# Spreading two sums of absolute values over heads 1 to 11 and splitting the rounding of the second weight, in a transformer layer on one core

## The chip, the cores and the metric

The kernel runs on one core of a Trainium2 chip. The core has five engines that run their own instruction streams and meet only at semaphores: PE (TensorE, matrix products into PSUM), ACT (ScalarE, activations), DVE (VectorE, elementwise work and reductions), POOL (GpSimd, elementwise work in SBUF) and SP (SyncE, here only an issuer of DMAs). POOL and ACT can issue DMAs too. Sixteen DMA engines move the data. The metric is the device time of one execution in microseconds (us).

## The reference

One layer over four sequences of 512 tokens of width 512: attention with 16 query heads of size 32 that share one key and one value head, a residual with layer norm, a gated feed-forward block whose three weights are rounded to -1, 0 or 1, and a residual with layer norm again.

```python
q = rotary((x @ Wq + bq) by heads);  k = rotary(x @ Wk + bk);  v = x @ Wv + bv
attn = softmax(q @ k.T / sqrt(32));   x = layernorm(x + (attn @ v) @ Wo + bo)

def quantize(w):
    gamma = mean(abs(w))                       # over the whole 1408 x 512 matrix
    return clip(round(w / (gamma + 1e-8)), -1, 1)

hidden = sigmoid(x @ quantize(w1).T) * (x @ quantize(w2).T)
x = layernorm(x + hidden @ quantize(w3).T)
```

What matters here is `quantize`: the sum of absolute values over a whole weight has to be known before its first element can be rounded.

## The kernel before

**Sequences and heads.** Sequence 0 runs through its 16 heads in `first_heads()` of each engine. A head is four score tiles of 128 x 512 (PE, line 1309), four row minima (DVE, 1021), four exponentials (ACT, 723), sixteen turns of 128 x 128 blocks (PE, 1337) and four copies of the turned tiles out of PSUM, two on ACT (751) and two on DVE (1042); the turns and copies of head h-1 lie inside head h. Every four heads make a group, whose context is summed a head later (PE, 1366). Sequences 1 to 3 run in `heads(b)`, in 32 steps k, two to a head; a step makes two score tiles, and around them the tables `BESIDE` and `LAST_BESIDE` place everything else: projections of the next queries, keys and values, the output projection, and the feed-forward block of the sequence before (`up0` to `up10`, `dn0` to `dn3`). From sequence 1 on the probabilities are cut into two 16-bit halves (ACT 744, DVE 1034, the latter in `p_low`) and turned by DMA transposes, one to a step, that SP issues (line 467, `turn`). They leave from four slots: the exponentials of step k wait for the transpose of step k-4.

**Weights.** `stage[0]` holds w1, `stage[1]` w2, and `stage[2]` is the same memory as `stage[0]` and takes w3. Each weight goes through three steps. ACT sums absolute values in four pieces of 128 x 1408 (`abs_sum(i)`, line 760; i from 0 to 3 is w1, 4 to 7 w2, 8 to 11 w3). PE adds the four partial sums over the partitions (`total(n)`, 1394) and DVE makes the threshold of it (`thresholds(n)`, 894 to 899). POOL rounds the weight in four pieces of three instructions each (`round_weight(n, c)`, 541, 543, 545); each piece raises the semaphore `rounded` by one. The tables `ABS_AT` and `TOTAL_AT` name the heads of sequence 0 at whose end the pieces 0 to 7 and the totals 0 and 1 stand. Pieces 8 to 11 stand in steps 4 to 7 of sequence 1, and the third total after step 8.

**POOL** also does the rotations (`rotation`: cosines 522, sines 527, sum 530), adds the output bias to the input rows (`add_bias`, 563), makes the inverse deviations (551 to 558), and from sequence 1 on issues the DMAs that stack the high and low halves of a head's queries (`stack`, 422; four DMAs a head). In sequence 0 SP issues those stacks.

**SP** runs in one order. Behind the stacks of sequence 0 it waits for all eight pieces of w1 and w2, then issues the rows of x (`load_x(0)`, line 453) and w3 (488), and behind these stand the transposes of sequence 1:

```python
sp.wait_ge(rounded, 2 * PIECES)
load_x(0)
sp.dma_start(stage[2], w3).then_inc(w_ffn[2], 16)
...
turn(b, *divmod(k - 1, PAIRS))      # line 467, sequence 1 onwards
```

The order inside POOL, SP, ACT, DVE and PE is written out by hand; no scheduler changes it.

Of the kernel before, what the change touches and what calls it, by code (L numbers as in the profile page):

```python
# [56 lines left out]
PIECES = 4  # L57
# [5 lines left out]

FIRST_Q_AT = [3, 7, 11, 15]
FIRST_Q = [(0, 2), (0, 3), (1, 0), (1, 1)]
ABS_AT = [0, 1, 1, 2, 3, 4, 5, 6]
TOTAL_AT = [3, 7]
FIRST_POOL_ROTATES = ("q1", "q2", "q3")
ROUND = 1.5 * 2.0 ** 23

# [131 lines left out]
def layer(nc, xT, x, wq, small, wo, b_rows, w1, w2, w3, table, out):  # L202
    with ExitStack() as ctx:
# [309 lines left out]
        def _(pool):  # L513
# [55 lines left out]
            pool.wait_ge(lo_done, unit_count(0, "k") + 1)  # L569
            rotation(0, "q1")  # L570
            rotation(0, "q2")
            pool.wait_ge(thr_step, 2)
            for c in range(PIECES):
                round_weight(0, c)
            rotation(0, "q3")
            pool.wait_ge(thr_step, 2 * 2)
            for c in range(PIECES):
                round_weight(1, c)
            rotation(1, "q0")
            cosines(1, "k")  # L580
            stack(pool, 1, 0)
            add_bias(0, 0)
            add_bias(0, 1)
            sines(1, "k")
            add_bias(0, 2)
            add_bias(0, 3)
            for h in range(1, HPG - 1):
                stack(pool, 1, h)
            for b in range(1, B):
                stack(pool, b, 3)  # L590
                if b > 1:
                    inverse_std(b - 2, 1, 2)
                rotation(b, "q1")
                if b > 1:
                    inverse_std(b - 2, 1, 3)
                stack(pool, b, 4)
                stack(pool, b, 5)
                rotation(b, "q2")
                stack(pool, b, 6)
                inverse_std(b - 1, 0, 0)  # L600
                inverse_std(b - 1, 0, 1)
                stack(pool, b, 7)
                inverse_std(b - 1, 0, 2)
                inverse_std(b - 1, 0, 3)
                if b == 1:
                    pool.wait_ge(thr_step, 2 * 3)
                    round_weight(2, 0, 0)
                    round_weight(2, 2, 1)
                stack(pool, b, 8)
                stack(pool, b, 9)  # L610
                rotation(b, "q3")
                if b == 1:
                    round_weight(2, 1, 2)
                    round_weight(2, 3, 3)
                add_bias(b, 0)
                stack(pool, b, 10)
                add_bias(b, 1)
                stack(pool, b, 11)
                add_bias(b, 2)
                add_bias(b, 3)  # L620
                for h in range(12, H):
                    stack(pool, b, h)
                if b < B - 1:
                    rotation(b + 1, "q0")
                if b < B - 1:
                    inverse_std(b - 1, 1, 0)
                    stack(pool, b + 1, 0)
                    stack(pool, b + 1, 1)
                    inverse_std(b - 1, 1, 1)
                    rotation(b + 1, "k")  # L630
                    stack(pool, b + 1, 2)
# [571 lines left out]
        def _(pe):  # L1203
# [146 lines left out]
            def first_context(g, blocks):  # L1350

                for k in blocks:
                    if k == 0:
                        if g == 0:
                            pe.wait_ge(kv_drained, 3)
                        if g < 2:
                            pe.wait_ge(total_read, g + 1)
                        if g == 2:
                            pe.wait_ge(kv_drained, 5)
                        pe.wait_ge(ctx_done, g)  # L1360
# [26 lines left out]
            def total(n):  # L1387

                pe.wait_ge(abs_summed, (n + 1) * SUMS)
                pe.wait_ge(ctx_done, n if n < 2 else HG)  # L1390
                if n == 0:
                    pe.wait_ge(ones_set, 1)
                    pe.wait_ge(kv_drained, 3)
# [204 lines left out]
```

## Time and profile before

| | |
|---|---|
| time, median of 3 runs (lowest to highest) | 607.18 us (606.84 to 608.12) |
| time of the profiled execution | 605.79 us |
| span of its instructions | 604.0 us |
| PE busy | 546.0 us, 90% of the span |
| DVE busy | 470.7 us, 78% |
| ACT busy | 426.0 us, 71% |
| POOL busy | 303.4 us, 50% |
| granted TensorE clock, mean | 0.974 of full |

The profiled execution took 1.4 us less than the median, and its span leaves out 1.8 us around the first and the last instruction. Busy shares are means over stages with different limits. Sequence 0's heads end at about 119 us in the span; the stage of interest runs from there to about 200 us. All times below are microseconds from the start of the span unless a duration is meant.

### The profile page before, as it was taken

Reading aid. Unit: us, or ns where it says so; the run is one execution under the profiler, and the core shown is the slowest. Engines: PE = TensorE matmul, PEld = TensorE weight load, DVE = VectorE, ACT = ScalarE, POOL = GpSimd, SP = SyncE. Lnnn points to the kernel's source line nnn. Section 1 sums busy time; section 2 is a strip of 40 time slices with the busy share of each in tenths; the row PEclk is TensorE's granted clock in tenths of the full one; section 3 lists DMA queues with packets and bytes.
Section 4 is the critical chain, followed back from the end, with each engine's and each line's share of the span. In section 5 each row is a group of like instructions: output and inputs, shape, how many; then the busy total and the mean of one; then the engine's idle time right before and its main releaser. Section 6 shows DMA issues by size and latency. Waiting matters only on the chain.

```text
span 604.0 us, 9187 instructions
## 1 busy us (share of the span) xinstructions
PE 546.0 (90%) x2984; PEld 273.0 (45%) x2984; DVE 470.7 (78%) x635; ACT 426.0 (71%) x865; POOL 303.4 (50%) x398
## 2 busy tenths in 40 slices
PE   9777989899789798999899989999599999989993
PEld 5443545444344344445444445354344444444441
DVE  2867878889989698888899898799989897444433
ACT  2697767789978587686888897687989796233300
POOL 2219696838599633958457325897453400201011
PEclk9789999999999899999899999999799999999997
DMA  8680428249989778999999987999899989100001
GB/s 307 189 307 17 123 49 301 54 81 191 215 182 180 159 151 134 163 199 197 213 200 190 191 161 140 176 188 197 171 218 167 183 165 195 41 1 36 1 0 69
DMA packets 217119, 92.12 MB, mean 153 GB/s; under 512 B 204400, under 2 KB 205552, under 8 KB 216560
## 3 DMA queue, kind: packets, MB, share of 16 engines
q1 hardware_dynamic: 209952, 77.61, 62.3%
q0 software_dynamic: 6144, 12.60, 10.1%
q10 hardware_dynamic: 976, 1.33, 0.6%
q8 instruction: 24, 0.39, 0.3%
q14 instruction: 23, 0.19, 0.1%
HBM read 20.20 MB, written 4.19 MB: 40 GB/s over the span
## 4 chain that ended last, share of the span: by engine, by line
PE 57%; DVE 13%; issue 9%; POOL 8%; ACT 7%; DMA 3%; SPq 2%; POOLq 0%; ACTq 0%; DVEq 0%
PE a_ps L1281 10%; PE b_ps L1281 6%; PE c_ps L1382 6%; PE s_ps L1294 6%; PE a_ps L1212 5%; PE e_ps L1281 5%; PE s_ps L1326 4%; DVE p_all L1034 3%; PE c_ps L1366 3%; PE b_ps L1294 2%; DVE sh_sb L1027 2%; POOL q_st L422 2%; PE b_ps L1266 2%; PE a_ps L1294 2%; PE s_ps L1337 2%
## 5 line engine op out<-in xcount | busy, mean ns | idle before, releaser
L736 ACT ACTIVATE p_all<-s_ps,sh_sb 128x512 f32<-128x512 f32 x192 | 130.1, 683 | 58.0 <-DVE sh_sb L1027 57.4
L1027 DVE TENSOR_REDUCE sh_sb<-s_ps 128x2 f32<-128x1024 f32 x96 | 116.7, 1215 | 23.8 <-PE s_ps L1326 23.7
L1034 DVE SCALAR_TENSOR_TENSOR p_all<-p_all 128x1024 f16<-128x1024 f32 x96 | 131.0, 1364 | 3.1 <-ACT p_all L744 3.0
L744 ACT ACTIVATE p_all<-p_all 128x1024 f16<-128x1024 f32 x96 | 101.7, 1060 | 2.0
L1281 PE MATMUL a_ps<-late,q 128*128 128x512 f16 x352 | 83.5, 380 | 3.2 <-DVE late L974 1.7
L1326 PE MATMUL s_ps<-k_st,q_st 128*128 128x512 f32 x192 | 79.2, 494 | 2.7 <-ACT p_all L736 1.6
L551 POOL TENSOR_SCALAR rstd<-mv 128x1 f32<-128x1 f32 x32 | 9.2, 287 | 136.6 <-DVE mv L994 136.4
L422 POOL DMA_DIRECT2D q_st<-hi x96 | 49.5, 518 | 51.9 <-PE s_ps L1326 28.2
L1212 PE MATMUL a_ps<-xT_sb,wq_sb 128*128 128x512 f32 x104 | 51.9, 625 | 4.9 <-DVE late L1013 4.1
L1281 PEld LDWEIGHTS a_ps<-late,q 128*128 128x128 fp8e4 x352 | 31.8, 98 | 45.9 <-issue 7.4
L422 POOL DMA_DIRECT2D q_st<-lo x96 | 47.4, 498 | 9.6 <-DVE lo L937 9.3
L723 ACT ACTIVATE p_all<-s_ps,sh_sb 128x512 f32<-128x512 f32 x48 | 33.0, 693 | 21.6 <-DVE sh_sb L1021 21.6
L1326 PEld LDWEIGHTS s_ps<-k_st,q_st 128*128 128x128 f32 x192 | 34.1, 191 | 28.9 <-issue 17.5
L1382 PE MATMUL c_ps<-pt_sb,vh 128*32 128x512 f16 x768 | 45.4, 391 | 1.1 <-DMA pt_sb<-p_all 1.1
L522 POOL TENSOR_TENSOR rot<-raw,table_sb 128x512 f32<-128x512 f32 x20 | 26.3, 1313 | 38.2 <-ACT raw L657 32.4
L1281 PE MATMUL b_ps<-late,q 128*128 128x512 f16 x192 | 45.4, 379 | 0.0
L527 POOL TENSOR_TENSOR rot<-rot,table_sb 128x512 f32<-128x512 f32 x18 | 23.9, 1331 | 35.2 <-DVE rot L906 34.9
L736 ACT ACTIVATION_READ_ACCUMULATOR p_all<-s_ps,sh_sb 128x1 f32 x192 | 37.8, 197 | 0.0
L1281 PE MATMUL e_ps<-late,q 128*128 128x512 f16 x160 | 37.8, 379 | 0.0
L1021 DVE TENSOR_REDUCE sh_sb<-s_ps 128x1 f32<-128x512 f32 x48 | 31.3, 681 | 6.4 <-PE s_ps L1309 6.4
L1294 PE MATMUL s_ps<-q,late 128*128 128x512 fp8e4 x154 | 34.1, 379 | 0.0
L1042 DVE COPY pt_sb<-e_ps 128x512 f32<-128x512 f32 x32 | 22.0, 688 | 14.2 <-PE e_ps L1337 14.2
(153 smaller groups left out, 995.1 us busy)
## 6 DMA issues: line engine op xcount, KB each, us to landing
q_st<-hi POOLq DMA_DIRECT2D x96, 64.0 KB, 3.6
q_st<-lo POOLq DMA_DIRECT2D x96, 64.0 KB, 4.1
late<-in_w SPq DMA_DIRECT2D x2, 2816.0 KB, 13.3
xT_sb<-in_xT SPq DMA_DIRECT2D x8, 512.0 KB, 5.5
late<-in_x SPq DMA_DIRECT2D x4, 1024.0 KB, 6.4
out<-late SPq DMA_DIRECT2D x12, 256.0 KB, 3.1
late<-in_w SPq DMA_DIRECT2D x2, 1408.0 KB, 7.1
q_st<-hi SPq DMA_DIRECT2D x32, 64.0 KB, 2.0
```

The costliest lines, as they stand in the source:

```text
L422: engine.dma_start(q_st[HD * r:HD * (r + 1), slot, :].bitcast(F32), half[HD * (h % HPG):HD * (h % HPG + 1), :].bitcast(F32)).then_inc(stac ...
L723: act.activation(p_sb[:, h % 2, t, :], first_bank(n), ACT.Exp, bias=sh_sb[:, n % (2 * PSLOTS):n % (2 * PSLOTS) + 1], scale=-1.0, accum_out ...
L736: act.activation(p_pair[n][:, t % 2, :], pair_banks(h * PAIRS + t // 2)[:, t % 2, :], ACT.Exp, bias=sh_sb[:, 2 * n + t % 2:2 * n + t % 2 + ...
L744: act.activation(p_half[n][:, 0, :], p_pair[n].rearrange("p t k -> p (t k)"), ACT.Copy, scale=P_SCALE).then_inc(p_hi, 1)
L1021: dve.tensor_reduce(sh_sb[:, n % (2 * PSLOTS):n % (2 * PSLOTS) + 1], first_bank(n), AX.X, ALU.min).then_inc(maxed, 1)
L1027: dve.tensor_reduce(sh_sb[:, 2 * n:2 * n + 2], pair_banks(h * PAIRS + i), AX.X, ALU.min).then_inc(maxed, 2)
L1034: dve.scalar_tensor_tensor(out=p_half[n][:, 1, :], in0=p_pair[n].rearrange("p t k -> p (t k)"), scalar=P_SCALE, in1=p_half[n][:, 0, :], op ...
L1212: mm = pe.matmul(wide_bank(name, s)[:, :], wq_sb[:, k, g * P:(g + 1) * P], xT_sb[:, k, :], start=(k == 0), stop=(k == DT - 1))
L1281: mm = pe.matmul(ps[:, :], w[:, k, f * P:(f + 1) * P], hT[:, n, k, :], start=(k == 0 and n == 0), stop=(k == DT - 1 and n == 1))
L1294: mm = pe.matmul(ps[:, :], gT[:, n, f, t * P:(t + 1) * P], q3v[:, f, :], start=(f == 0 and n == 0), stop=(f == FT - 1 and n == 1))
L1326: pe.matmul(pair_banks(n)[:, t % 2, :], q_st[:, slot, t * P:(t + 1) * P], k_st[:, b % 2, :], start=True, stop=True).then_inc(scored, 1)
L1382: mm = pe.matmul(c_ps[HD * j:HD * (j + 1), :], vh[:, m, k, :], pt_half[:, (b * H + g * HPG + j) % PTR, :, n, :, k, :], start=(k == 0 and n ...
```

## The change

Four things are edited. The pieces 0 to 7 of the sums of absolute values stand at the ends of heads 1, 3, 5, 6, 8, 9, 10 and 11 instead of 0, 1, 1, 2, 3, 4, 5 and 6. The totals stand at the ends of heads 7 and 11 instead of 3 and 7, with the waits that this order needs (contexts 1 and 2 wait for the totals in place of contexts 0 and 1; total 1 waits for the keys' bank). POOL rounds w1 behind the rotation of q3 rather than ahead of it. And POOL rounds one piece of w2 behind the key's sines of sequence 1, and three pieces behind the stacks of heads 1 and 2 of that sequence, with the four bias additions moved behind the next rotation.

```diff
-ABS_AT = [0, 1, 1, 2, 3, 4, 5, 6]
-TOTAL_AT = [3, 7]
+ABS_AT = [1, 3, 5, 6, 8, 9, 10, 11]
+TOTAL_AT = [7, 11]
...
             rotation(0, "q2")
+            rotation(0, "q3")
             pool.wait_ge(thr_step, 2)
             for c in range(PIECES):
                 round_weight(0, c)
-            rotation(0, "q3")
-            pool.wait_ge(thr_step, 2 * 2)
-            for c in range(PIECES):
-                round_weight(1, c)
             rotation(1, "q0")
             cosines(1, "k")
             stack(pool, 1, 0)
-            add_bias(0, 0)
-            add_bias(0, 1)
             sines(1, "k")
-            add_bias(0, 2)
-            add_bias(0, 3)
+            pool.wait_ge(thr_step, 2 * 2)
+            round_weight(1, 0)
             for h in range(1, HPG - 1):
                 stack(pool, 1, h)
+            for c in range(1, PIECES):
+                round_weight(1, c)
             for b in range(1, B):
                 stack(pool, b, 3)
...
                 rotation(b, "q1")
...
+                if b == 1:
+                    add_bias(0, 0)
+                    add_bias(0, 1)
                 stack(pool, b, 4)
+                if b == 1:
+                    add_bias(0, 2)
+                    add_bias(0, 3)
                 stack(pool, b, 5)
...
-                        if g < 2:
-                            pe.wait_ge(total_read, g + 1)
+                        if g in (1, 2):
+                            pe.wait_ge(total_read, g)
...
-                pe.wait_ge(ctx_done, n if n < 2 else HG)
+                pe.wait_ge(ctx_done, n + 1 if n < 2 else HG)
+                if n == 1:
+                    pe.wait_ge(kv_drained, 5)
```

On POOL, between the key's cosines of sequence 1 and the rotation of its q1, the order before is this (`late` is the staged weight or the rows of x, `b_sb` the bias, `q` the rounded weight, `rot` the tile being rotated):

```order
L422 DMA q_st<-lo 32x512 x2
L563 TENSOR_TENSOR late<-late,b_sb 128x512 x2
L527 TENSOR_TENSOR rot<-rot,table_sb 128x512
L530 TENSOR_TENSOR rot<-rot 128x512
L563 TENSOR_TENSOR late<-late,b_sb 128x512 x2
```

And after, in the same place:

```order
+L527 TENSOR_TENSOR rot<-rot,table_sb 128x512
+L530 TENSOR_TENSOR rot<-rot 128x512
+L541 TENSOR_SCALAR late<-late,thr 128x1408
+L543 TENSOR_SCALAR late<-late 128x1408
+L545 TENSOR_SCALAR q<-late 128x1408
+L422 DMA q_st<-hi 32x512 x2
+L422 DMA q_st<-lo 32x512 x2
+L422 DMA q_st<-hi 32x512 x2
+L422 DMA q_st<-lo 32x512 x2
+L541 TENSOR_SCALAR late<-late,thr 128x1408
+L543 TENSOR_SCALAR late<-late 128x1408
+L545 TENSOR_SCALAR q<-late 128x1408
```

Two more such pieces of three follow before the stack of head 3. The rounding of w2, which stood ahead of all this, now stands inside it, and SP's wait for it goes with it.

On PE, between heads 11 and 12 of sequence 0, the order before has the key's sum (1443) and then the scores of head 12 at once:

```order
L1212 MATMUL a_ps<-xT_sb,wq_sb 128x512
L1443 MATMUL c_ps<-th,table_sb 128x512
L1309 MATMUL s_ps<-k_st,q_st 128x512 x3
L1309 MATMUL b_ps<-k_st,q_st 128x512
L1337 MATMUL s_ps<-table_sb,p_all 128x128 x4
```

After, the total of the absolute sums stands between them (lines on PE read 3 to 5 higher):

```order
L1215 MATMUL a_ps<-xT_sb,wq_sb 128x512
L1448 MATMUL c_ps<-th,table_sb 128x512
L1399 MATMUL c_ps<-asum,ones 128x4
L1312 MATMUL s_ps<-k_st,q_st 128x512 x3
L1312 MATMUL b_ps<-k_st,q_st 128x512
L1340 MATMUL s_ps<-table_sb,p_all 128x128 x4
```

The total needs the piece that ACT sums at the very end of head 11, so the scores of head 12 now stand behind ACT's whole head 11.

## Rows read from the trace of the kernel before

**Rows 1.** The chain that ended last, 158 to 210 us: start, us, what.
```profile
158.69 0.57 POOL rstd L554
159.62 1.42 POOL late L541
...
171.37 0.62 POOL q_st L422
...
189.14 1.37 POOL q L545
...
204.98 4.84 PE c_ps L1382 x56
```

**Rows 2.** ACT's timeline in sequence 0: start, us, instruction [idle before <-releaser].
```profile
28.79 1.38 ACT L760 ACTIVATE q<-late 128x1408 fp8e4<-128x1408 f32 x1
...
30.42 1.38 ACT L760 ACTIVATE q<-late 128x1408 fp8e4<-128x1408 f32 x1 [0.16 <-DMA late<-in_w]
...
37.77 0.69 ACT L723 ACTIVATE p_all<-s_ps,sh_sb 128x512 f32<-128x512 f32 x1 [0.88 <-DVE sh_sb L1021]
...
43.69 0.70 ACT L723 ACTIVATE p_all<-s_ps,sh_sb 128x512 f32<-128x512 f32 x1
...
83.59 0.69 ACT L723 ACTIVATE p_all<-s_ps,sh_sb 128x512 f32<-128x512 f32 x1 [2.37 <-DVE sh_sb L1021]
...
94.36 0.69 ACT L723 ACTIVATE p_all<-s_ps,sh_sb 128x512 f32<-128x512 f32 x1
```

**Rows 3.** SP's timeline: w2 issued, then a stack of head 4.
```profile
24.80 0.45 SPq L478 DMA_DIRECT2D late<-in_w  x1
...
29.75 1.22 SPq L422 DMA_DIRECT2D q_st<-lo  x2
```

**Rows 4.** Landing, w2 (line 478); then stacks issued from 30.2 to 31 us.
```profile
DMA to landing us min/median/max: 12.7/12.7/12.7
...
DMA to landing us min/median/max: 8.2/8.8/9.3
```

**Rows 5.** PE's timeline: the first total, then head 4's scores.
```profile
41.01 0.28 PE L1394 MATMUL c_ps<-asum,ones 128*128 128x4 f32 x2
41.15 0.94 PE L1309 MATMUL s_ps<-k_st,q_st 128*128 128x512 f32 x3
```

**Rows 6.** DVE's timeline: minima behind the first total; a lower half.
```profile
41.79 1.27 DVE L1021 TENSOR_REDUCE sh_sb<-s_ps 128x1 f32<-128x512 f32 x2
...
56.52 1.82 DVE L937 TENSOR_TENSOR lo<-rot,hi 128x512 fp32r<-128x512 f32 x1
```

**Rows 7.** POOL's timeline, first piece of w1, last of w2, then the hand-over to sequence 1.
```profile
47.54 1.45 POOL L541 TENSOR_SCALAR late<-late,thr 128x1408 f32<-128x1408 f32 x1
...
51.87 1.44 POOL L541 TENSOR_SCALAR late<-late,thr 128x1408 f32<-128x1408 f32 x1
...
90.10 1.37 POOL L545 TENSOR_SCALAR q<-late 128x1408 int8<-128x1408 f32 x1
...
108.64 1.28 POOL L530 TENSOR_TENSOR rot<-rot 128x512 f32<-128x512 f32 x1
...
117.45 0.99 POOL L422 DMA_DIRECT2D q_st<-lo  x2
```

**Rows 8.** SP's timeline: rows of x, w3, and the first transposes of sequence 1.
```profile
92.73 0.58 SPq L453 DMA_DIRECT2D late<-in_x  x1
93.36 0.53 SPq L488 DMA_DIRECT2D late<-in_w  x1
126.51 21.86 SPq L467 DMA_TRANSPOSE pt_sb<-p_all  x6
```

**Rows 9.** Landing of w3 (line 488).
```profile
DMA to landing us min/median/max: 13.9/13.9/13.9
```

**Rows 10.** ACT's timeline in sequence 1: step 2, step 4, and step 4's piece of w3.
```profile
131.23 0.61 ACT L666 ACTIVATE hi<-rot 128x512 fp32r<-128x512 f32 x1
...
135.10 0.68 ACT L736 ACTIVATE p_all<-s_ps,sh_sb 128x512 f32<-128x512 f32 x1
...
137.53 1.36 ACT L760 ACTIVATE q<-late 128x1408 fp8e4<-128x1408 f32 x1
```

**Rows 11.** Stages: us, busy of PE, PEld, DVE, ACT, POOL, clock, DMA, GB/s.
```profile
140.00:150.00 10.00, 10.00 (x27) 4.92 (x26) 9.72 (x18) 9.39 (x19) 9.03 (x15) 1.00 1.12 211
```

**Rows 12.** DMA queues and issues, 130 to 160 us.
```profile
q1 hardware_dynamic: 14168, 4.55, 87.5%
...
pt_sb<-p_all SPq DMA_TRANSPOSE x8, 5.9
```

## The prediction

> **What bounds the kernel now.** I read the chain that ended last first, then the timelines of the engines it names, and last the landing times of the DMAs they wait for. The page says that PE is busy for 90% of the span, but the change does not touch PE's work, so the question is where something else holds PE up. The chain answers it for the start of sequence 1: from 158.69 to past 189 us it is almost wholly POOL, which rounds w3 there and stacks queries in between, and only at 204.98 does it return to PE [rows 1]. What starts that stretch of POOL is w3's threshold, and that hangs on ACT's four pieces of w3 in steps 4 to 7, the first at 137.53 [rows 10]. ACT has no room around them: from 140 to 150 us it is busy 9.39 of 10 us [rows 11]. So whatever delays ACT at step 4 delays the threshold, POOL, and then PE, and nothing later gives it back. In sequence 0 heads alternate between ACT, DVE and PE; rows have to be read head by head.
>
> **Part 1, the sums leave heads 0 to 4.** Eight pieces of 1.4 us move; none is removed, so this gains only where ACT is last. Head 1 had two pieces, at 28.79 and 30.42, the second 0.16 us late for the other half of w1 [rows 2]. With one left, head 2 starts 1.6 us earlier. Head 2 loses its piece as well, ahead of head 3's start at 37.77, which waited on DVE then [rows 2]; another 0 to 1.5 us. Piece 0 of head 0 gains nothing, since head 1 then waits for slow turns on PE. But head 4 cannot use it all. Its stacked queries are behind w2: w2 was issued at 24.80 and took 12.7 us, to 37.5, and stacks issued at about 30.4 behind it took up to 9.3 us, to 39.7 [rows 3, 4]. Their issue waits on DVE and does not move. Head 4's scores started at 41.15 [rows 5], so they gain at most 1.4 us, and its exponentials (43.69) gain 1.7 to 2.7 us, the rest being the total that stood ahead. Head 5 has a lower half that took 1.82 us on DVE [rows 6] while POOL rounded; with POOL idle there now it falls nearer to 0.7, for 1.1 us. Gain by head 6: 2.8 to 3.8 us.
>
> **Part 2, the sums enter heads 8 to 11.** In heads 8 and 9 ACT ended with idle time, 2.37 us ahead of head 10 [rows 2], and a piece of 1.4 us fits. Head 10 has about 0.5 us of room, so it costs 0.9. Head 11 is the costly one. ACT ran without a gap into head 12 at 94.36 [rows 2]. Now it sums a piece first (1.4 us), and only then may PE make total 1 and behind it the scores of head 12, which ran ahead of ACT before. From a total to the minima took 41.01 to 41.79 plus one reduction of 0.64 [rows 5, 6], 1.4 us. So head 12 starts 0.9 + 1.4 + 1.4 = 3.7 us later, of which some 0 to 0.9 is slack at head 13, where DVE was last. Cost: 2.8 to 3.8 us. **Sequence 0 ends where it did, within 1 us.** I take 0.
>
> **Part 3, when w2 is rounded.** Before, its last piece ended at 90.10 + 1.37 = 91.5 [rows 7]. Now no piece may start before the key's sum, which ends at 108.64 + 1.28 = 109.9 [rows 7] and which DVE's shuffle in head 13, not POOL, times. A piece takes 4.33 us (47.54 to 51.87) [rows 7]. The order behind it is one piece, 4.3; the stacks of heads 1 and 2, two of the three heads that took six pairs of about 0.99, so 4.0 [rows 7]; three pieces, 13.0. That gives 109.9 + 4.3 + 4.0 + 13.0 = 131.2. Beside DVE's work of sequence 1 two pieces of w3 took 159.62 to 171.37, 11.75 us where 8.7 is free of it [rows 1]. From 118 to 125 DVE has little to do, so I add 1.3 us for the last two pieces: **w2 is rounded at 132.5**, with 131 and 135 as ends.
>
> The Trainium skill (SBUF — State Buffer, Who interferes with whom) says that POOL and a DVE instruction with two SBUF inputs exclude each other for a whole instruction. Three lower halves of the probabilities would then cost POOL up to 3.6 us, an estimate, and put the rounding at the 135 end; the rows show a smaller excess for the same mix.
>
> **Part 4, who waits for it.** SP waits for exactly these eight pieces. Queued behind are the rows of x, w3, and then every transpose of sequence 1. Before, x left at 92.73 and w3 at 93.36, and w3 took 13.9 us, so both were there long before the first transpose at 126.51 [rows 8, 9]. That cover is gone. Now x leaves at 132.6, w3 at 133.2, w3 lands at 133.2 + 13.9 = 147.1, and the first transpose is issued at about 134 instead of 126.5.
>
> - ACT's piece of w3 in step 4 stood at 137.53 [rows 10]. It cannot start before 147.1: 9.6 us late.
> - ACT's exponentials of step 4 (135.10 [rows 10]) wait for the first transpose. That lies in SP's queue behind 3.9 MB. The stacks behind w2 landed only when w2 had [rows 4], so I expect the same here. A transpose then costs its own share of the DMA engines: eight of them filled most of 87.5% of 30 us [rows 12], some 3 us each. Step 4 starts at 147.1 + 3.0 = 150.1, **15.0 us late**, and the wait of the piece vanishes in it.
> - ACT's high half in step 2 (131.23 [rows 10]) waits for POOL's next rotation, which with the last pieces at 132.5, a stack of 2.0 and 3.9 us of rotation ends at 138.4. ACT is 7 us late there, and this is hidden in the same 15.0.
> - The bias additions, 1.3 us each, wait for x now, which lands near 139; they end by 146 and hold up nobody who is not already waiting.
>
> From step 4 on ACT has its former pace, 3.9 to 5.1 us a step, and the three transposes that wait behind the first come 3 us apart, ahead of it. So w3's threshold comes 15 us later, and POOL's chain and all behind it too. The sum on the profiled execution is 605.8 + 15.0 = 620.8; the median of the runs stands 1.4 higher, so **622.2 us**, 2.5% slower. Ends for the main case: rounding at 131 or 135, transpose share 2 to 5 us, sequence 0 off by 1 either way, up to 1 us regained: 618 to 627.
>
> **Rivals.**
>
> - *Transposes pass the loads.* If SP's later DMAs do not have to wait for w3, ACT is held only by w3 itself: 607.2 + 9.6 = 616.8, or 615 with the rounding at 131. For it: x issued first does not hold its followers in any row. Against it: the stacks behind w2. The Trainium skill (DMA: Bandwidth & Descriptors, Queues, rings and completion order) says both that a ring's descriptors are consumed in order and that completion is not first in, first out for an issuing engine. By the former 622 stands, by the latter 617.
> - *The loads meet a full DMA.* The DMA share was 1.12 from 140 to 150 us [rows 11]. If the late loads, POOL's stacks and four transposes at a time stretch each other, w3 lands 3 to 5 us later still and steps 5 to 8 wait again: 627 to 632.
> - *Faster.* If ACT's early relief were not stopped by head 4's queries, sequence 0 would end up to 3.8 us earlier, and if POOL's chain from 158.69 had as much room as ACT is late, the rest would be hidden: 607.2 - 3.8 = 603.4. It decides by whether the threshold of w3 can come 15 us later without POOL waiting. The chain has no gap there, so I give it little.
> - *Nothing.* Loads and pieces hidden altogether, 607: it needs w3 to land by 137.5, that is the rounding at 123, which POOL's own 21.3 us from 109.9 exclude unless sequence 0 runs 8 us ahead.
>
> **How the numbers follow.** Main case 0.66; transposes pass 0.13; full DMA 0.15; faster 0.03; nothing 0.03. The range of 615 to 628 leaves out the two last, most of the full-DMA case and little else, close to 2 in 10. What a measurement can tell from no change is about 0.2%, 1.2 us: faster 0.03, same 0.02, slower 0.95.
>
> **What the profile after would show.** Right: ACT's exponentials of head 12 near 98; POOL's last instruction on w2 ending at 131 to 135; SP's x and w3 directly behind it; ACT idle for about 10 us ahead of step 4 with a DMA named as its releaser; w3's threshold near 174; PE idle around 140 to 150, perhaps with a lower granted clock behind it. Wrong: step 4 starting before 145, or POOL's chain behind the threshold shorter than the 39 us it took. If the time is under 612, the chain through w3 had slack that I did not see.

## The result: 3.2% slower, and the profile after

In one comparison the changed kernel took 626.40 us (median of 4 runs, 624.03 to 628.54) where the kernel before took 607.01 (4 runs, 605.27 to 608.12). The ratio is 1.0315, 95% interval [1.0275, 1.0355]. The forecast of 622.2 had the sign, the place and most of the size; some 4 us more came than it said (19.4 against 15.0).

The profiled execution has a span of 623.4 us, 19.4 more than before. First the busy times of its engines, then its stages. A line of the second view gives the stretch, its length, the busy time of PE, PEld, DVE, ACT and POOL, the granted clock, the DMA share and GB/s:

```profile
PE 548.3 (88%) x2984; PEld 272.8 (44%) x2984; DVE 475.3 (76%) x635; ACT 426.4 (68%) x865; POOL 305.1 (49%) x398
```

```profile
0.00:119.00 119.00, 99.44 (x530) 57.73 (x530) 85.77 (x143) 81.45 (x191) 50.56 (x51) 0.96 0.42 135
...
140.00:150.00 10.00, 0.00 (x0) 0.00 (x0) 1.83 (x2) 2.99 (x7) 4.46 (x7) 0.55 1.05 331
...
142.00:158.00 16.00, 3.55 (x7) 2.26 (x8) 8.50 (x9) 8.00 (x15) 10.39 (x14) 0.50 1.10 259
```

No engine's sum of busy time grew by more than 5 us, so most of what came is idle time. From 140 to 150 us PE does nothing, where it was busy for all 10 us before [rows 11], and the clock it is granted is about half (0.55). Three marks, two on ACT and one on POOL, say how the 19.4 us came. Sequence 1 starts at 119.43 (before 119.04), w3's first piece is rounded at 178.54 (before 159.62 [rows 1]), and what is left of the span from there is 444.9 us (before 444.4). So nearly all of it, 18.5 us, lies between 119 and 178 us. ACT's timeline there, as in [rows 10]:

```profile
146.98 0.63 ACT L669 ACTIVATE hi<-rot 128x512 fp32r<-128x512 f32 x1 [15.26 <-DMA q_st<-lo]
...
150.58 0.69 ACT L739 ACTIVATE p_all<-s_ps,sh_sb 128x512 f32<-128x512 f32 x1
...
153.02 1.36 ACT L763 ACTIVATE q<-late 128x1408 fp8e4<-128x1408 f32 x1
...
157.44 0.69 ACT L739 ACTIVATE p_all<-s_ps,sh_sb 128x512 f32<-128x512 f32 x1 [2.96 <-DVE sh_sb L1030]
...
162.37 0.69 ACT L739 ACTIVATE p_all<-s_ps,sh_sb 128x512 f32<-128x512 f32 x1 [1.04 <-DVE sh_sb L1030]
```

The high half of step 2 waits 15.26 us for a DMA, the stack of head 3. Step 4 follows at 150.58 without a wait of its own, 15.5 us later than before; step 5 at 157.44 waits for DVE and is 18.4 us late, step 6 is 19.0 late, and from there the distance stays. What led up to it is on POOL, SP and in the landing times, which answer to [rows 7 to 9]. POOL's last instruction on w2 and the stack of head 3:

```profile
132.09 2.22 POOL L545 TENSOR_SCALAR q<-late 128x1408 int8<-128x1408 f32 x1
134.26 1.07 POOL L422 DMA_DIRECT2D q_st<-hi  x2
135.32 0.99 POOL L422 DMA_DIRECT2D q_st<-lo  x2
```

SP's loads and the transposes behind them:

```profile
134.34 0.40 SPq L453 DMA_DIRECT2D late<-in_x  x1
134.77 0.51 SPq L488 DMA_DIRECT2D late<-in_w  x1
135.67 29.73 SPq L467 DMA_TRANSPOSE pt_sb<-p_all  x6
```

The landing of w3, of the transposes issued from 130 to 160 us, and of POOL's stacks up to 137 us:

```profile
DMA to landing us min/median/max: 13.8/13.8/13.8
...
DMA to landing us min/median/max: 5.7/6.6/14.8
...
DMA to landing us min/median/max: 1.8/2.1/11.1
```

w2 was rounded at 134.31. Behind it SP's two loads left, w3 landed at 148.6 and the first transpose at 135.67 + 14.8 = 150.5. The stack of head 3, on POOL's own queue, was issued at the same moment as the loads and landed at 146.9, 11.1 us after its issue. The stacks issued before 119 us landed in about 2, and those that the kernel before issued beside its transposes, from 133 to 137 us, in 3.8 to 6.1. The high half of the next four heads may not be written before that stack has read the old one, so ACT stood in step 2. Step 4's own wait, for the first transpose, ran out at 150.5, just as ACT came to it.

The 3.5 us between steps 4 and 6 are DVE's and PE's. DVE first, then PE:

```profile
147.71 0.69 DVE L940 TENSOR_TENSOR lo<-rot,hi 128x512 fp32r<-128x512 f32 x1 [14.63 <-ACT hi L669]
...
150.07 3.71 DVE L1037 SCALAR_TENSOR_TENSOR p_all<-p_all 128x1024 f16<-128x1024 f32 x1 [0.53 <-ACT p_all L747]
...
154.02 0.29 DVE L950 TENSOR_REDUCE vmax<-v_sb 128x1 f32<-128x128 f32 x1
```

```profile
154.45 0.56 PE L1253 MATMUL e_ps<-vmax,ones 128*128 128x1 f32 x2 [17.11 <-DVE vmax L950]
154.87 1.20 PE L1329 MATMUL s_ps<-k_st,q_st 128*128 128x512 f32 x2
155.87 4.67 PE L1269 MATMUL a_ps<-wo_sb,cx 128*128 128x512 f32 x8
```

POOL's second pair of bias additions ran from 150.19 to 152.69, and the lower half of the probabilities that DVE began at 150.07 took 3.71 us instead of 1.21. The maximum of the values stands behind it on DVE, PE's in-order stream stands behind that maximum, and with it the scores of step 5. PE had then idled for 17.11 us and worked at half clock: two score tiles took 1.20 us and wo1, eight matmuls of the output projection, 4.67 instead of 3.59. The second pair of additions ran so late because it stands behind head 4's stack, which waits for the high half of step 2.

### The profile page after: what moved, and what is told of

Read it like the earlier page. It is cut to its first block, busy times and chain, and to the rows that moved or that the text cites. A ratio compares the mean times of both kernels' runs of the same rounds, so it can differ in the third digit from the quotient of the medians.

```text
span 623.4 us, 9187 instructions
## 1 busy us (share of the span) xinstructions
PE 548.3 (88%) x2984; PEld 272.8 (44%) x2984; DVE 475.3 (76%) x635; ACT 426.4 (68%) x865; POOL 305.1 (49%) x398
## 4 chain that ended last, share of the span: by engine, by line
PE 52%; DVE 14%; POOL 12%; issue 8%; ACT 7%; DMA 6%; SPq 0%; POOLq 0%; ACTq 0%; DVEq 0%
PE a_ps L1284 10%; PE c_ps L1385 5%; PE s_ps L1297 5%; PE b_ps L1284 5%; DVE p_all L1037 4%; PE e_ps L1284 4%; PE s_ps L1329 4%; DMA q_st<-lo 4%; PE a_ps L1215 3%; PE b_ps L1297 3%; POOL q_st L422 3%; DVE sh_sb L1030 2%; POOL q L545 2%; POOL late L543 2%; POOL late L541 2%
## 5 line engine op out<-in xcount | busy, mean ns | idle before, releaser
L1037 DVE SCALAR_TENSOR_TENSOR p_all<-p_all 128x1024 f16<-128x1024 f32 x96 | 135.3, 1409 | 2.9 <-ACT p_all L747 2.8
L1030 DVE TENSOR_REDUCE sh_sb<-s_ps 128x2 f32<-128x1024 f32 x96 | 116.6, 1215 | 24.3 <-PE s_ps L1329 24.2
L563 POOL TENSOR_TENSOR late<-late,b_sb 128x512 f32<-128x512 f32 x16 | 25.1, 1582 | 14.6 <-DMA late<-in_x 14.4
```

Source lines behind the costliest of these rows:

```text
L1030: dve.tensor_reduce(sh_sb[:, 2 * n:2 * n + 2], pair_banks(h * PAIRS + i), AX.X, ALU.min).then_inc(maxed, 2)
L1037: dve.scalar_tensor_tensor(out=p_half[n][:, 1, :], in0=p_pair[n].rearrange("p t k -> p (t k)"), scalar=P_SCALE, in1=p_half[n][:, 0, :], op ...
```

## Experiments

Each ratio below is to the kernel before, run in the same comparison; its median there was between 605.2 and 608.2 us. The profiled execution is one of the runs. The step marks are read from it, and so are the differences between them.

**One side of the change alone.** The kernel before with POOL's new order, and the sums where they were:

```diff
+            rotation(0, "q3")
             pool.wait_ge(thr_step, 2)
             for c in range(PIECES):
                 round_weight(0, c)
-            rotation(0, "q3")
...
             sines(1, "k")
-            add_bias(0, 2)
-            add_bias(0, 3)
+            pool.wait_ge(thr_step, 2 * 2)
+            round_weight(1, 0)
...
+            for c in range(1, PIECES):
+                round_weight(1, c)
```

> The kernel before with POOL's new order alone: sums and totals stay at their old heads, w1 is rounded behind the rotation of q3 and w2 in one piece and three pieces around the stacks of sequence 1. Theory A (the loss is the rounding of w2 that ends at 134 instead of 91, by what SP queues behind it): w2 is rounded at 134 +- 1 again, and the time is 625 to 627.5. Theory C (the new places of the sums, with total 1 ahead of head 12's scores, bring part of the loss): 618 to 623.

622.98 us (621.23 to 624.99), ratio 1.0278 [1.0223, 1.0332]. Sequence 0 ended at 116.40, w2 was rounded at 131.30, step 4 came at 147.17, and w3's rounding at 175.01. Theory A missed the time by 2 us; it fell just inside theory C's range. Most of the loss is POOL's order: from the end of sequence 0 to w3's rounding this run lost 18.0 us, the changed kernel 18.5. The sums' new places add about 3 us to sequence 0 (119.43 against 116.40); by the times alone the two intervals overlap.

**The load of w3 taken from behind w2's rounding.** The changed kernel, with:

```diff
+            sp.wait_ge(rounded, PIECES)
+            sp.dma_start(stage[2], w3).then_inc(w_ffn[2], 16)
             sp.wait_ge(rounded, 2 * PIECES)
             load_x(0)
-            sp.dma_start(stage[2], w3).then_inc(w_ffn[2], 16)
```

> The changed kernel, but SP issues w3 as soon as w1's four pieces are rounded (about 88 us); only the rows of x still wait for w2. Theory A (2.9 MB of w3 between the rounding and everything else): head 3's stack lands within 5 us instead of 11.1, ACT's high half in step 2 starts when POOL's rotation ends, at 140 to 141 instead of 146.98, step 4 at about 144.5 instead of 150.6, and the time is 615 to 619. Theory B (POOL's lateness costs it all, the loads only ride along): step 2's wait ends where it did and the time stays at 625 to 628.

619.58 us (618.66 to 622.10), ratio 1.0217 [1.0171, 1.0264]: w3's load in that place costs some 6 to 7 us of the 19. Theory A fits, though step 2 came 1 us and the time 0.6 us above its ranges; theory B falls. ACT's steps 2, 4 and 5:

```profile
142.12 0.63 ACT L670 ACTIVATE hi<-rot 128x512 fp32r<-128x512 f32 x1 [11.01 <-DMA q_st<-lo]
...
145.65 0.68 ACT L740 ACTIVATE p_all<-s_ps,sh_sb 128x512 f32<-128x512 f32 x1
...
152.57 0.69 ACT L740 ACTIVATE p_all<-s_ps,sh_sb 128x512 f32<-128x512 f32 x1 [3.03 <-DVE sh_sb L1031]
```

Step 4 is still 10.6 us late. POOL's own delay leaves that much even with no weight on the way: head 3's stack is issued at 133.7 to 135.2 and lands 4.7 to 6.8 us later beside x and the transposes. Step 4 waited for no transpose here: they landed at most 8.5 us after their issue at 134.51, so the stack alone held ACT. The extra of step 5 is there too.

**Late loads alone.** The kernel before, with w2 rounded early as ever, and x and w3 held back until the rotation of sequence 1's q1; the bias additions stand as in the changed kernel, since they need x:

```diff
             sp.wait_ge(rounded, 2 * PIECES)
+            sp.wait_ge(rotated, unit_count(1, "q1") + 1)
             load_x(0)
```

> The kernel before with the loads of x and w3 held on SP until the rotation of q1 of sequence 1 (about 130 us), and the four bias additions moved behind that rotation as in the change; rounding and sums as before. Theory A: w3 lands at 144 to 145, the first transpose behind it at 146 to 147, ACT's step 4 starts 11 to 12 us late, its step 2 on time; 618 to 622. Theory B: 607 to 609.

618.92 us (616.65 to 621.32), ratio 1.0200 [1.0150, 1.0251]. ACT's steps 2 and 4:

```profile
130.87 0.61 ACT L669 ACTIVATE hi<-rot 128x512 fp32r<-128x512 f32 x1
...
148.82 0.69 ACT L739 ACTIVATE p_all<-s_ps,sh_sb 128x512 f32<-128x512 f32 x1 [13.97 <-DMA pt_sb<-p_all]
```

Step 2 is on time, since no stack is caught, and step 4 waits for the first transpose, issued at 130.89 and landing 17.8 us later (w3 took 12.3). The time is in theory A's range, step 4 a little later than it said (13.7 us late). So loads ahead of the transposes are enough for a loss of 11 us, with POOL's rounding where it was.

This run also tells what the half clock does. It has no extra between steps 4 and 6: step 6 came 7.93 us behind step 4, where the kernel before took 8.32 and the changed kernel 11.79. Yet PE had been idle for 9.59 us and was granted half the clock from 144 to 157 us, and eight matmuls took 5.97 us. ACT's step 6 and PE's rows:

```profile
156.75 0.67 ACT L739 ACTIVATE p_all<-s_ps,sh_sb 128x512 f32<-128x512 f32 x1
```

```profile
150.32 1.22 PE L1329 MATMUL s_ps<-k_st,q_st 128*128 128x512 f32 x2 [9.59 <-ACT p_all L739]
152.74 5.97 PE L1215 MATMUL e_ps<-xT_sb,wq_sb 128*128 128x512 f32 x8 [1.20 <-DVE power L955]
```

Here the maximum of the values and the scores of step 5 had been made before the wait, at 135.94 and 136.59. So the low clock alone did not delay ACT's steps here; in the changed kernel PE's work for step 5 still stood behind DVE's stretched lower half.

**Another queue for w3.** The changed kernel with w3 issued by POOL behind head 3's stack:

```diff
                 stack(pool, b, 3)
+                if b == 1:
+                    pool.wait_ge(rounded, 2 * PIECES)
+                    pool.dma_start(stage[2], w3).then_inc(w_ffn[2], 16)
```

> The changed kernel, but w3 is issued by POOL, directly behind head 3's stack, instead of by SP; it leaves some 2 us later. Theory A: the stack is ahead of w3 in its queue now and ACT's step 2 starts at 140 to 142; the first transpose is not behind w3 any more and lands by 147; ACT's piece of w3 in step 4 becomes the last wait, at 150 to 152 instead of 137.53 of the kernel before, 13 to 14.5 us late; 619 to 623. If a load on another queue holds the transposes as much as one ahead of them: 625 to 628.

629.91 us (627.28 to 633.01), ratio 1.0383 [1.0322, 1.0444], the slowest of all and above both expectations. ACT again, then the landings of w3 and of the transposes:

```profile
148.98 0.63 ACT L671 ACTIVATE hi<-rot 128x512 fp32r<-128x512 f32 x1 [17.69 <-DMA q_st<-lo]
...
159.10 0.69 ACT L741 ACTIVATE p_all<-s_ps,sh_sb 128x512 f32<-128x512 f32 x1 [6.50 <-DMA pt_sb<-p_all]
```

```profile
DMA to landing us min/median/max: 19.9/19.9/19.9
...
DMA to landing us min/median/max: 7.7/10.7/24.3
```

With the weight on POOL's queue the first transpose landed 24.3 us after its issue, the stack, now ahead of w3 in the same queue, after up to 13.5 us, and w3 after 19.9. A place behind w3 in SP's queue is therefore not needed to hold the transposes: beside this 2.9 MB load all of them were slow, and the transpose slower than when it stood behind the load (24.3 against 14.8). The Trainium skill (DMA: Bandwidth & Descriptors, Queues, rings and completion order) says that each DMA engine takes turns between the queues that have work. The trace agrees in that a load on one queue slows the other (24.3 us); how the turns are shared out, and why a transpose fared worse so, no run here shows.

**The bias additions.** The changed kernel with all four ahead of head 4's stack, so that none runs beside step 3's lower half:

```diff
                 if b == 1:
-                    add_bias(0, 0)
-                    add_bias(0, 1)
+                    for t in range(TT):
+                        add_bias(0, t)
                 stack(pool, b, 4)
-                if b == 1:
-                    add_bias(0, 2)
-                    add_bias(0, 3)
```

> The changed kernel with all four bias additions ahead of head 4's stack, where POOL stands idle for 5.5 us, instead of two behind it. In the changed kernel DVE's lower half of step 3 took 3.71 us instead of 1.21 beside the two late additions (150.19 to 152.69). Theory D (the two engines hold each other up there, and that makes 2.5 of the 19 us): the lower half takes 1.2 to 1.5 us, step 5 starts 2 to 3 us earlier relative to step 2, the time is 2 to 3 us below the changed kernel, 623.5 to 624.5. Rival (step 5 waits for its transpose from the backlog in any case): step 5 no earlier by more than 0.5 us, 626 to 627.

623.79 us (620.98 to 625.82), ratio 1.0262 [1.0223, 1.0301]. DVE's lower half of step 3, and ACT's step 5:

```profile
149.19 1.23 DVE L1034 SCALAR_TENSOR_TENSOR p_all<-p_all 128x1024 f16<-128x1024 f32 x1 [0.53 <-ACT p_all L744]
```

```profile
156.20 0.69 ACT L736 ACTIVATE p_all<-s_ps,sh_sb 128x512 f32<-128x512 f32 x1 [2.55 <-DMA pt_sb<-p_all]
```

The addition was what stretched it (1.23 against 3.71 us), as theory D said. But step 5 now waited for its transpose, to 10.10 us after step 2 instead of 10.46, as the rival said. By w3's rounding 1.5 us of the extra were regained, 30.0 against 31.6 us behind step 2. The time is in theory D's range, but its interval overlaps the changed kernel's, and the two profiled executions took the same 625.2 us, so no gain in the whole time is shown. The Trainium skill (SBUF — State Buffer, Who interferes with whom) says that a DVE instruction with two SBUF inputs contends with a GpSimd instruction that reads SBUF, for ports held by an exclusive lock. The trace agrees in the length: 3.71 us is what two additions (2.50) and the instruction (1.21) take one after the other. DVE's instruction was the first to start there, by 0.12 us, and waited all the same.

**Head 3's stack first.** The changed kernel with that stack ahead of the last three pieces of w2:

```diff
-            for h in range(1, HPG - 1):
+            for h in range(1, HPG):
                 stack(pool, 1, h)
             for c in range(1, PIECES):
                 round_weight(1, c)
             for b in range(1, B):
-                stack(pool, b, 3)
+                if b > 1:
+                    stack(pool, b, 3)
```

> The changed kernel, with head 3's stack issued by POOL ahead of the last three pieces of the second weight instead of behind them. Theory (two waits of ScalarE end together: one for this stack in step 2, one for the first transposes in step 4): step 2's high half comes at 140 to 141 instead of 146.98, but step 4's exps stay at 149.5 to 151, because the first transpose still lands near 150.5. VectorE is further ahead, so step 5 comes up to 3 us earlier. Time 622 to 624.5 us. Rival (the stack's late landing alone held ScalarE, the transposes only filled the time): step 4's exps at about 144.5, time 616 to 618.5 us.

626.68 us (625.11 to 627.01), ratio 1.0321 [1.0285, 1.0356]: no gain. ACT's steps 2 and 4:

```profile
139.35 0.63 ACT L670 ACTIVATE hi<-rot 128x512 fp32r<-128x512 f32 x1 [8.26 <-POOL rot L530]
...
154.42 0.69 ACT L740 ACTIVATE p_all<-s_ps,sh_sb 128x512 f32<-128x512 f32 x1 [11.44 <-DMA pt_sb<-p_all]
```

The wait of 15.26 us for the stack, the largest in the trace of the changed kernel, is gone, and the time is the same. Step 4 waits for the transpose instead, to 154.42, later than the 149.5 to 151 that I expected: the transpose was issued 1.2 us later and took 17.4 us to land instead of 14.8. Both expectations missed the time; the rival, by which the stack alone was the cause, missed it by over 8 us and falls. The theory's two waits are there, but the later landing hides what the stack's removal alone is worth, and from step 4 to w3's rounding this run took 25.9 us, the changed kernel 28.0. Why the landing grows when nothing holds ACT in step 2 I did not settle. It was also 17.8 in the run with late loads alone, where step 2 was on time.

**The sums one head earlier**, so that none ends head 11 (the changed kernel, one line):

```diff
-ABS_AT = [1, 3, 5, 6, 8, 9, 10, 11]
+ABS_AT = [1, 3, 5, 6, 7, 8, 9, 10]
```

> The changed kernel with the last four sums at heads 7, 8, 9 and 10 instead of 8 to 11, total 1 still behind head 11. Head 12's scores no longer wait for a sum at the end of head 11. My price for that place (1.4 us of sum on the path) gives the exponentials of head 12 about 1.4 us earlier relative to head 11, but head 7 has no idle time and costs 1 to 1.4: sequence 0 ends 0 to 1.5 us earlier, time 625 to 626.5. Rival (the whole 3.7 us that I priced for heads 10 to 12 hangs on that sum): 3 to 4 us earlier, 622.5 to 623.5.

625.54 us (6 runs, 623.02 to 632.31), ratio 1.0265 [1.0228, 1.0301]. Head 12 came 6.70 us behind head 11 instead of 7.99, 1.3 us earlier for 1.4 priced, so the rival's 3 to 4 us fall. But sequence 0 ended at 120.72, later than 119.43, where 0 to 1.5 us earlier was expected: heads 7, 9 and 10 lost 3.0 us, heads 11 and 12 gave 2.3. The profiled execution took 632.31, the longest of the six, and the difference of 0.9 us in the medians decides nothing.

**Rounding spread over sequence 0's last heads.** Two kernels. Pieces of w2 stand between the halves of rotations and behind stacks, from 94 to 125 us, and w3 is loaded early:

```diff
-            rotation(1, "q0")
+            cosines(1, "q0")
+            pool.wait_ge(thr_step, 2 * 2)
+            round_weight(1, 0)
+            sines(1, "q0")
             cosines(1, "k")
             stack(pool, 1, 0)
+            round_weight(1, 1)
             sines(1, "k")
-            pool.wait_ge(thr_step, 2 * 2)
-            round_weight(1, 0)
+            round_weight(1, 2)
             for h in range(1, HPG - 1):
                 stack(pool, 1, h)
-            for c in range(1, PIECES):
-                round_weight(1, c)
+            round_weight(1, 3)
```

With the sums of the changed kernel:

> The sums and totals as in the change, w1 rounded behind the rotation of q3, but w2's four pieces earlier: one between cosines and sines of sequence 1's q0, one behind its head 0's stack, one behind the key's sines, one behind the stacks of heads 1 and 2; and SP issues w3 behind w1's rounding. Theory A (all the loss is in what the late rounding holds up): w2 rounded at 121 to 125, no wait of ACT in step 2, step 4 within 1 us of 135.1, and the time is within 1.5 us of the kernel before: 606 to 609. Rival (sums at heads 8 to 11 cost by themselves): 610 or more.

With the sums of the kernel before:

> As the run with the spread rounding and early w3, but sums and totals at the heads of the kernel before. In the run with the late rounding alone sequence 0 ended at 116.4 instead of 119.04, which I put down to POOL being idle beside DVE in heads 4 to 6. If that gain is kept, 604 to 605.5; if the pieces of w2 in heads 11 to 14 take it back by holding up DVE there, 606.5 to 608.

614.07 us (612.80 to 615.31), ratio 1.0105 [1.0073, 1.0137], and 613.57 (612.87 to 614.34), ratio 1.0097 [1.0072, 1.0122]. The times miss the first run's theory A and both ranges of the second. The first run's rival named the range but not the reason, since with the old sums the time is the same: here their place makes no difference. About 13 of the 19 us are back, and part of what is left shows the same hold-up on DVE. In the first of the two, DVE's lower half of step 3 and POOL's additions:

```profile
139.24 3.94 DVE L1040 SCALAR_TENSOR_TENSOR p_all<-p_all 128x1024 f16<-128x1024 f32 x1
```

```profile
139.60 2.49 POOL L564 TENSOR_TENSOR late<-late,b_sb 128x512 f32<-128x512 f32 x2
```

Sequence 0 ends 2.7 and 3.3 us late, at 121.74 and 122.35.

**Attempts to beat both.** Sums at the ends of heads 1, 2, 4, 5, 6, 7, 8 and 8, totals at 7 and 9, w3 early, stacks 1 to 3 and then all four additions ahead of q1's rotation, and w2's pieces between 86.8 and 114.9 us:

```diff
-ABS_AT = [1, 3, 5, 6, 8, 9, 10, 11]
-TOTAL_AT = [7, 11]
+ABS_AT = [1, 2, 4, 5, 6, 7, 8, 8]
+TOTAL_AT = [7, 9]
...
-            rotation(1, "q0")
+            pool.wait_ge(thr_step, 2 * 2)
+            round_weight(1, 0)
+            cosines(1, "q0")
+            round_weight(1, 1)
+            sines(1, "q0")
             cosines(1, "k")
             stack(pool, 1, 0)
+            round_weight(1, 2)
             sines(1, "k")
-            pool.wait_ge(thr_step, 2 * 2)
-            round_weight(1, 0)
+            round_weight(1, 3)
...
```

> An attempt to beat both kernels. All of the second weight's rounding is put into sequence 0's last steps, in pieces between rotations and key parts, after the sums of absolute values have been taken in heads 1 to 8; the third weight's load is issued behind the first weight's rounding; the four bias additions follow stacks 1 to 3 together. Theory (what costs time is only the work of POOL that delays stacks and loads, and VectorE held beside the bias additions): sequence 0 ends at 117 (115.5 to 118.5), the second weight is rounded by about 115, the lower half of step 3 takes 1.2 to 1.5 us, and the time is 603 to 608 us, 605 the likeliest. Rival (pieces of rounding beside VectorE's instructions in heads 11 to 14 take the gain back, as in the two runs with spread pieces): sequence 0 ends at 120 or later, time 608 to 612 us.

609.29 us (12 runs, 604.63 to 613.41) beside 606.00 for the kernel before, ratio 1.0043 [1.0009, 1.0078]. It is the rival's range. w2 is rounded at 114.90 as expected, but sequence 0 ends at 121.14, 2.1 us late and 4 later than the theory said; step 4 comes at 137.89, 2.8 late. Head 12 began 2.65 us ahead of the kernel before and head 13 level with it, because DVE waits in order for q0's rotation, which a piece had pushed back:

```profile
99.51 0.43 DVE L938 CAST hi<-rot 128x512 fp32r<-128x512 f32 x1 [2.43 <-POOL rot L531]
```

Next that piece went behind q0's sines:

```diff
-            cosines(1, "q0")
+            rotation(1, "q0")
             round_weight(1, 1)
-            sines(1, "q0")
```

> The attempt before this one with one piece of the second weight moved from between the cosines and sines of sequence 1's q0 to behind them. There VectorE waited 2.43 us for that rotation in head 12, which took 10.5 us instead of 8.1, and head 13 lost the 2.65 us that head 12 had been ahead. Theory (the rotation kept waiting is what cost the lead): head 13 starts at 99.8 to 100.8 instead of 102.25, sequence 0 ends at 118 to 119.5 instead of 121.14, time 604 to 606.5 us, 0.0 to 0.5% under the kernel before. Rival (the lead is lost in heads 13 to 15 to the other pieces and a lower TensorE clock): head 13 at 100 too, but sequence 0 ends at 120.5 or later, time 608 to 610 us.

610.56 us (11 runs, 607.11 to 615.97), ratio 1.0058 [1.0027, 1.0089]. Head 13 came at 101.50, and in head 14 DVE waited for the key's rotation, behind the next piece; sequence 0 ended at 122.76. Both expectations missed: head 13 wasn't near 100, and the time is above either range.

```profile
112.52 0.43 DVE L928 CAST k_st<-rot 128x512 fp32r<-128x512 f32 x1 [2.68 <-POOL rot L531]
```

Last, that piece too:

```diff
-            round_weight(1, 2)
             sines(1, "k")
+            round_weight(1, 2)
             round_weight(1, 3)
```

> The last attempt, with the second weight's third piece moved from ahead of the key's sines of sequence 1 to behind them, so that no piece stands between VectorE's shuffle and the rotation that it waits for next. In the run before VectorE waited 2.68 us there in head 14, and sequence 0 ended at 122.76. Theory (what takes the lead back is VectorE waiting in order for a rotation that a piece of rounding delays): no such wait in heads 12 to 14, head 15 starts at 111.5 to 113 instead of 115.47, sequence 0 ends at 117.5 to 119.5, time 603.5 to 607 us, level with the kernel before or up to 0.5% faster. Rival (pieces anywhere in heads 12 to 15 cost by holding single instructions of VectorE): sequence 0 ends at 120.5 or later, time 608 to 611 us.

Sequence 0 ended at 118.33, inside the expected 117.5 to 119.5 and 0.7 us before the kernel before. The time was 614.64 us all the same, above both ranges (6 runs, 611.20 to 615.82), ratio 1.0143 [1.0100, 1.0187]. POOL, then ACT in step 2:

```profile
125.04 6.54 POOL L564 TENSOR_TENSOR late<-late,b_sb 128x512 f32<-128x512 f32 x4 [1.21 <-DMA late<-in_x]
131.55 2.30 POOL L523 TENSOR_TENSOR rot<-raw,table_sb 128x512 f32<-128x512 f32 x1
```

```profile
136.45 0.63 ACT L668 ACTIVATE hi<-rot 128x512 fp32r<-128x512 f32 x1 [5.36 <-POOL rot L531]
```

The theory held in sequence 0 and failed for the time. ACT now reached step 2 before the rotation of q1, which stands behind the additions, and those began at 125.04 instead of 121.80 in the first attempt and took 6.54 us beside DVE's lower halves instead of 5.16. So the cover for POOL's 17 us is missing somewhere in each of these orders. None was faster than the kernel before, which rounds w2 from 73.50 to 91.5 without a gap or another task of POOL's in between.

## Why the prediction was right, and by how much it was off

**What bounds.** Right. w3's rounding went from 159.62 to 178.54, 18.9 us, and the span grew by 19.4: a delay of that chain came through whole, which was what decided the sign. "Nothing later gives it back" holds only to some 3 us: from w3's rounding to the end the traces took 441.9 us (late loads alone) to 447.3 (the additions together), the kernel before 444.4.

**Part 1, relief in sequence 0.** Head 6 began 4.15 us earlier (54.82 against 58.97) where I had 2.8 to 3.8. But much of it wasn't the sums'. With the sums where they were and only POOL's order changed, head 6 began at 56.09, so 1.3 us are theirs in that comparison, and at head 4 it was 1.2 (40.92 against 42.11), where I had 1.7 to 2.7. The lower half of head 5, 1.82 us beside POOL's rounding [rows 6], took 0.69 without it, as the prediction had it. And heads 2 and 3 ran at a lower granted clock in the trace of before than in that of after (0.79 and 1.00 from 30 to 38 us). The rows are of the kernel before and of the one with only POOL's order changed, which was granted 1.00 as well:

```profile
30.00:38.00 8.00, 6.00 (x25) 3.90 (x23) 3.90 (x7) 6.97 (x17) 0.00 (x0) 0.79 0.96 376
```

```profile
30.00:38.00 8.00, 5.63 (x28) 3.21 (x27) 5.39 (x9) 7.83 (x19) 0.00 (x0) 1.00 0.97 366
```

These two kernels are the same up to there, so 1 to 1.5 us of a head's start may differ between executions, and I had read it as time of the sums.

**Part 2, the cost in heads 8 to 11.** From head 9 to head 12 it was 22.35 us instead of 18.89, 3.5 us against the 3.7 forecast, by the mechanism named: 0.7 in head 10 (0.9 forecast) and 2.7 in head 11 (2.8). PE, where the total waits for ACT's piece:

```profile
92.08 0.38 PE L1399 MATMUL c_ps<-asum,ones 128*128 128x4 f32 x2 [2.21 <-ACT q L763]
92.32 0.94 PE L1312 MATMUL s_ps<-k_st,q_st 128*128 128x512 f32 x3
```

Another 0.9 us went in head 12. Sequence 0 ended at 119.43 against 119.04, within the 1 us. This zero was a gain and a cost that cancel: alone, POOL's order ends the sequence at 116.40, so the sums' places were about 3 us worse there, and I had them at nothing. The low clock in the trace of before helps the zero too, by the 1 to 1.5 us of part 1. That the end came out within 1 us is partly luck.

**Part 3, when w2 is rounded.** 134.31 against 132.5, inside 131 to 135. The term that was small is the hold-up beside DVE: the last three pieces took 118.74 to 134.31, 2.6 us over 13.0, where I had 1.3. Three instructions took 2.2 us instead of 1.4. My own row was nearer than the number that I took: it has 11.75 - 8.7 = 3.1 us of excess for two pieces, and I had cut it to 1.3 on an argument ("DVE has little to do") that holds for the first of the three pieces, 4.4 us long, and not for the other two. The rule of the Trainium skill (SBUF — State Buffer, Who interferes with whom), put at up to 3.6 us, was also nearer than 1.3.

**Part 4, who waits.** Forecast: x 132.6, w3 133.2 landing at 147.1, step 4 at 150.1. Measured: 134.34, 134.77, 148.6, 150.58. Step 4 is right to 0.5 us, but not by the wait that I had forecast. ACT did not idle ahead of it with a transpose as the releaser; it idled ahead of step 2, for a stack, and reached step 4 at 150.58 when the first transpose had just landed, at 150.5. That both ended together is luck, and so is that the loads came 1.6 us late and the transpose 1.9 us behind w3 instead of 3.0 (6.4 behind it in the late loads alone). The forecast wait itself is real: late loads alone held step 4 by it to 148.82. One sentence was wrong in its reason: step 2 at 138.4, held by POOL's rotation. It came at 146.98, held by a stack whose landing I hadn't counted. Its 2.0 us were POOL's issue alone, and I had applied "stacks behind a load land late" only to SP's queue. It added next to nothing to step 4, where the transpose landed at the same moment. The sign "head 12 near 98" was a slip: it leaves out part 1's own gain, 94.36 + 3.7 - 3.3 is 94.8, and 93.67 was measured.

**The step that failed** is "from step 4 on ACT has its former pace", with up to 1 us regained. Between steps 4 and 6 ACT lost 3.5 us more. The bias additions were to end by 146 and hold up nobody who is not already waiting. But the second pair stood behind head 4's stack, and with it behind step 2, ended at 152.69 and held DVE for 2.5 us exactly when ACT's wait ended. PE, idle for 17 us before it, then worked at half clock until about 158. Taking the additions away gave 1.5 us back by w3's rounding. The late loads alone, with step 2 on time and the same half clock, lost nothing between steps 4 and 6, so the extra belongs to the order in which work waits behind step 2, and the clock adds to it only where PE's scores stand on that path. How the rest divides between the clock, the first transposes and DVE's queue is open. With 18.9 instead of 15.0 the sum would be 607.2 + 18.9 = 626.1, against 626.4 measured.

**Rivals.** That transposes pass the loads falls by every run with w3 late: the first transpose landed behind w3 each time, even from another queue (159.0 against 155.8). That the loads meet a full DMA was half right: the DMA share was 1.05 from 140 to 150 us and the stack was stretched, but w3 took only 13.8 us. The measured 626.4 is next to its 627, but not by its mechanism: w3 landed 1.5 us later than forecast, not 3 to 5, and steps 5 and 6 waited for DVE.

## To carry to other kernels

When a producer is moved later, follow everything that its completion lets go: here a wait on SP released two loads, and the stack and the transpose issued within 2 us of them, on two queues, took 11.1 and 14.8 us to land. After a long wait, look at what all engines do in its first microseconds, since work that was parked meets there just as the critical engine resumes. And taking away the longest wait shown need not shorten anything: here a wait of 15.26 us went, another ended no earlier, and the time stayed.

## What the hardware showed that I had not expected

- A stack of 64 KB transfers on POOL's queue took up to 11.1 us to land beside a load on SP's queue, instead of about 2 in a quieter stretch and 3.8 to 6.1 beside transposes. With the load on POOL's queue a transpose on SP's took 24.3 us.
- SP itself was held. Its first transpose behind the loads occupied it for 12.68 us before it could issue the next, where those of the kernel before, from 126 to 150 us, took 1.8 to 6.6.
- After PE's 17.11 us without work the granted clock was 0.50 from 142 to 158 us, though PE worked again from 154.45. Eight matmuls of wo1 took 4.67 us from 155.87 on, and in the late loads alone, where the clock was 0.50 to 157 us, eight of the next queries took 5.97 from 152.74 on. At full clock both take 3.6.
- DVE's instruction with two SBUF inputs took as long as itself and two back-to-back additions of POOL together, 3.71 and 3.94 us instead of 1.2, although it had started before them, by 0.12 and 0.36 us.
